# Two cross attentions of a Perceiver kernel: three score banks that small users borrow, row sums moved between engines, and a last head that ends by columns

## The reference, cut to what matters

```python
s = (q_h @ k_h.T) * scale            # 512 queries x 8192 keys; layer 0 also masks keys
p = exp(s - rowmax(s))
att_h = (p @ v_h) / rowsum(p)        # rowsum is called the denominator below
x = x + concat(att_h) @ Wo.T + bo
```

## Time and profile before

| | us |
|---|---|
| median of 3 runs | 4286.01 |
| lowest and highest | 4283.99, 4290.52 |
| the profiled execution's own time | 4285.99 |
| its span, first to last instruction | 4284.3 |
| PE busy | 3842.7 (90% of the span) |
| DVE busy | 2908.2 (68%) |
| ACT busy | 2380.9 (56%) |
| POOL busy | 1754.6 (41%) |

### The profile page before, as it was taken

The page is one execution under the profiler, slowest core; times in us unless marked ns, Lnnn a source line. Parts: engine busy times, 40 slices in busy tenths (PEclk is TensorE's granted clock), DMA queues, the critical chain, the costliest instruction groups (busy, mean ns, idle before and its releaser), DMA issues. The chain is left out here.

```text
span 4284.3 us, 51332 instructions
## 1 busy us (share of the span) xinstructions
PE 3842.7 (90%) x17864; PEld 2216.7 (52%) x17864; DVE 2908.2 (68%) x3503; ACT 2380.9 (56%) x3635; POOL 1754.6 (41%) x1064
## 2 busy tenths in 40 slices
PE   7998999999999677788999589999999988769996
PEld 6886444444444242366888344444444335447885
DVE  4333878778787269756888477877778644468886
ACT  2223777777777544225777146666666630337775
POOL 0000587787788639600000236666666630000001
PEclk9998999999999889889999689999999988779998
DMA  8996566666666520025889456666666541308886
GB/s 313 327 338 218 128 156 155 148 156 149 153 153 149 130 89 0 10 84 210 325 324 337 145 132 155 148 151 153 142 153 150 115 102 40 70 32 329 325 321 242
DMA packets 294234, 745.22 MB, mean 174 GB/s; under 512 B 55486, under 2 KB 89022, under 8 KB 259418
## 3 DMA queue, kind: packets, MB, share of 16 engines
q1 hardware_dynamic: 246522, 570.48, 39.7%
q0 software_dynamic: 47456, 171.46, 19.8%
HBM read 476.62 MB, written 99.48 MB: 134 GB/s over the span
## 5 line engine op out<-in xcount | busy, mean ns | idle before, releaser
L794 ACT ACTIVATE prob<-psum 128x512 f32<-128x512 f32 x1552 | 891.4, 595 | 430.5 <-PE psum L693 393.0
L963 POOL TENSOR_TENSOR den_pool<-den_pool,prob 128x1024 f32<-128x1024 f32 x372 | 938.6, 2523 | 221.7 <-DVE den_pool L881 189.7
L693 PE MATMUL psum<-q_stack,k_ring 98*128 98x512 f32 x2048 | 1006.0, 509 | 19.8 <-ACT prob L794 14.3
L852 DVE CUSTOM_DVE_ANT_0 psum<-psum,mask_q 128x1024 f32<-128x1024 f32 x512 | 626.4, 1234 | 222.7 <-PE psum L655 208.8
L848 DVE TENSOR_REDUCE row_max<-psum 128x1 f32<-128x1024 f32 x512 | 615.2, 1219 | 235.5 <-PE psum L655 232.3
L655 PE MATMUL psum<-k_ring,q_stack 96*128 96x512 f32 x2048 | 677.5, 414 | 62.6 <-DVE row_max L848 26.9
L693 PEld LDWEIGHTS psum<-q_stack,k_ring 98*128 98x128 f32 x2048 | 394.6, 193 | 617.3 <-ACT prob L794 274.5
L1984 DVE TENSOR_TENSOR weight_lo<-weight_raw,weight_hi 128x2048 fp32r<-128x2048 f32 x240 | 548.3, 2289 | 133.3 <-ACT weight_hi L1927 132.5
L711 PE MATMUL psum<-prob,x 128*32 128x512 f32 x3104 | 514.6, 609 | 0.9 <-ACT prob L794 0.9
L1927 ACT ACTIVATE weight_hi<-weight_raw 128x2048 fp32r<-128x2048 f32 x240 | 457.0, 1917 | 71.7 <-DMA weight_raw<-in_L_ffn_w 36.8
L655 PEld LDWEIGHTS psum<-k_ring,q_stack 96*128 96x128 f32 x2048 | 386.8, 196 | 152.9 <-issue 61.4
(11 more groups left out here) (428 smaller groups left out, 6420.6 us busy)
## 6 DMA issues: line engine op xcount, KB each, us to landing
weight_raw<-in_L_ffn_w SPq DMA_DIRECT2D x120, 1024.0 KB, 6.8
den_dma<-prob POOLq DMA_DIRECT2D x204, 512.0 KB, 4.9
k_ring<-k_hi SPq DMA_DIRECT2D x1024, 64.0 KB, 2.1
weight_raw<-in_L_ffn_Wu SPq DMA_DIRECT2D x60, 1024.0 KB, 7.4
weight_raw<-in_L_ffn_Wd SPq DMA_DIRECT2D x60, 1024.0 KB, 6.6
den_dma<-xnT POOLq DMA_DIRECT2D x68, 512.0 KB, 4.9
k_ring<-k_lo SPq DMA_DIRECT2D x512, 64.0 KB, 2.2
ctxT<-in_ctxT SPq DMA_DIRECT2D x16, 1024.0 KB, 9.5
```

The source lines that it names most:

```text
L693: e.matmul(k.bank(b % 2), k_ring[:, n % kring, kt * P:(kt + 1) * P], q_stack[h % n_q][:], start=not masked, stop=True, skip_group_check=ma ...
L794: e.activation(prob[b // 2 % n_p][:, b % 2, :], k.bank(b % 2), ACT.Exp, scale=scale).then_inc(s_exp, 1)
L852: e.tensor_tensor_reduce(out=max_banks(q), in0=max_banks(q), in1=masks[0][:, i, 2 * c2 * KC:2 * (c2 + 1) * KC], scale=1.0, scalar=-3.0e38, ...
L963: e.tensor_tensor(den[:], den[:], tile, ALU.add).then_inc(s_dpool, 1)
```

## The change

In its own words: "Cross attention: three score banks, shared with PE's sums of six tiles a head in layer 1, where VectorE adds none; last head's sums by PE; its end by columns". A class `Banks` hands out banks 0, 1 and 7 in order of use. Blocks rotate over three; while `out` (`head_out`), `sums` (the new `sum_wave`) or `rows` (`max_rows`) holds one, blocks have two: blocks 22 to 25, in layer 1 also 30 to 41, and 60 to 63 of each head. Waves are all of four value products again, 16 a head. In layer 1 each of waves 6, 7 and 8 is followed by a group of four products with ones; ScalarE takes their bank into `den_pe` (`take_sums`); VectorE adds no tiles there; transfers carry 9 tiles in place of 8, POOL 17 in place of 13, and the ring of `prob` tiles has 16 in place of 10. In the last head of either layer PE also sums the last four waves. The final projection is split around `head_out` and its last quarter follows four reciprocals of 128 columns each. The diff, cut:

```diff
+WAVES = KT // 4
+OUT_STEP, OUT_BACK = 10, 26
+ROWS_STEP, ROWS_BACK = PAIRS - 3, KT
...
+class Banks:
+    def __init__(self, banks, first, sums):
+        self.bank, self.user_before = {}, {}
+        self.free_at, self.used = dict.fromkeys(banks, 0), {n: -3 + j for j, n in enumerate(banks)}
+        self.user = dict.fromkeys(banks)
+        self._take(("rows", 0), 0, 0, first)
+        for b in range(H * KT):
+            h, t = divmod(b, KT)
+            waves = sums.pe_waves(h)
+            if t == 2 * OUT_STEP + 2 and h > 0:
+                self._take(("out", h - 1), b, KT * h + OUT_BACK)
+            if waves and t == 2 * wave_step(waves[0]) + 2:
+                self._take(("sums", h), b, KT * h + 2 * wave_step(waves[-1]) + 6 if h + 1 < H else KT * H + 1)
+            if t == 2 * ROWS_STEP + 2 and h + 1 < H:
+                self._take(("rows", h + 1), b, KT * h + ROWS_BACK)
+            self._take(("block", b), b, 0)
+        self._take(("out", H - 1), H * KT, 0)
+    def _take(self, user, b, back, n=None):
+        if n is None:
+            n = min((n for n in self.user if self.free_at[n] <= b), key=lambda n: self.used[n])
+        self.bank[user], self.user_before[user] = n, self.user[n]
+        self.user[n], self.free_at[n], self.used[n] = user, back, b
...
+    def pe_waves(self, h):
+        return self.waves if h + 1 < H else self.last_waves
+    def by_dma(self, h):
+        return self.dma_tiles if h + 1 < H else self.last_dma_tiles
+    def by_pool(self, h):
+        return [p for p in range(PAIRS) if p not in self.by_dve and p not in self.by_dma(h) and p // 2 not in self.pe_waves(h)]
...
-    n_q, n_p = 3, 7 if masked else 10
+    n_q, n_p = 3, 7 if masked else 16
...
-        sums = Sums([0, 1, 2, 3, 4], [], list(range(5, PAIRS - 2, 3)))
+        sums = Sums([0, 1, 2, 3, 4], [], list(range(5, PAIRS - 2, 3)), [12, 13, 14, 15], [5, 8, 11, 14, 17, 20, 23])
     else:
-        sums = Sums([0, 1, 2, 3, 4], [12, 15, 18, 21, 24, 27], [7, 10, 13, 16, 19, 22, 25, 29])
-    waves = Waves(sums.by_pe)
+        sums = Sums([], [6, 7, 8], [1, 4, 7, 10, 19, 22, 25, 28, 30], [6, 7, 8, 12, 13, 14, 15], [1, 4, 7, 10, 19, 22])
+    banks = Banks((0, 1, 7), 7, sums)
...
+    def wait_for_bank(e, kind, n):
+        if banks.user_before[kind, n] is None:
+            return
+        kind, n = banks.user_before[kind, n]
+        if kind == "block":
+            e.wait_ge(s_exp, n + 1)
+        elif kind == "out":
+            e.wait_ge(s_dsum, n + 1)
+        elif kind == "sums":
+            e.wait_ge(s_pesum, pe_sums(n))
+        else:
+            e.wait_ge(s_mlo, n + 1)
...
-                elif b >= 2:
-                    e.wait_ge(s_exp, b - 1)
+                else:
+                    wait_for_bank(e, "block", b)
...
+                if w in sums.pe_waves(h):
+                    sum_wave(h, w)
+            def sum_wave(h, w):
+                first, last = sums.pe_waves(h)[0], sums.pe_waves(h)[-1]
+                if w == first:
+                    wait_for_bank(e, "sums", h)
+                for n in range(4):
+                    t = 4 * w + n
+                    ins = e.matmul(bank_of("sums", h)[n * DH:(n + 1) * DH, :], k.ones[:, 0:DH],
+                                   prob[(PAIRS * h + t // 2) % n_p][:, t % 2, :], start=w == first, stop=w == last,
+                                   skip_group_check=True)
+                ins.then_inc(s_sumw, 1)
...
+                if sums.pe_waves(h):
+                    e.wait_ge(s_pesum, pe_sums(h))
+                    e.matmul(out[3 * DH:4 * DH, :], k.ones[:, 0:DH], den_pe, start=True, stop=True)
...
+            def project(i):
+                matmuls(e, k.bank(2 + i), [(attT[:, c, i * P:(i + 1) * P], wo[:, c, :]) for c in range(DT - 1)],
+                        stop=False)
+            project(0)
+            project(1)
+            head_out(H - 1)
+            project(2)
+            project(3)
             for i in range(TT):
-                matmuls(e, k.bank(i), [(attT[:, c, i * P:(i + 1) * P], wo[:, c, :]) for c in range(DT - 1)],
-                        stop=False)
-            head_out(H - 1)
-            e.wait_ge(s_rec, 8 * (H // 4 - 1) + 2)
-            for i in range(TT):
-                e.matmul(k.bank(i), attT[:, DT - 1, i * P:(i + 1) * P], wo[:, DT - 1, :], start=False, stop=True
+                e.wait_ge(s_rec, 8 * (H // 4 - 1) + 2 * i + 2)
+                e.matmul(k.bank(2 + i), attT[:, DT - 1, i * P:(i + 1) * P], wo[:, DT - 1, :], start=False, stop=True
...
+            def take_sums(h):
+                if h > 0:
+                    e.wait_ge(s_head, h)
+                e.wait_ge(s_sumw, sums.pe_done(h, sums.pe_waves(h)[-1]))
+                e.activation(den_pe, bank_of("sums", h), ACT.Copy, scale=1.0 / DH).then_inc(s_pesum, 1)
...
+                if h + 1 < H and sums.waves and p == wave_step(sums.waves[-1]):
+                    take_sums(h)
...
-                e.tensor_tensor(den4[g, :], den4[g, :], misc[2 * DH:3 * DH, :], ALU.add).then_inc(s_dsum, 1)
+                out = bank_of("out", h)
+                if sums.pe_waves(h):
+                    e.tensor_tensor(den4[g, :], den4[g, :], out[3 * DH:4 * DH, :], ALU.add).then_inc(s_dhalf, 1)
+                    e.wait_ge(s_dhalf, pe_sums(h))
+                e.tensor_tensor(den4[g, :], den4[g, :], out[2 * DH:3 * DH, :], ALU.add).then_inc(s_dsum, 1)
...
-            reciprocal(H // 4 - 1, 0, slice(0, T))
-            divide(H // 4 - 1, 8 * (H // 4 - 1) + 1, slice(0, T))
+            for i in range(TT):
+                reciprocal(H // 4 - 1, 0, slice(i * P, (i + 1) * P))
+                divide(H // 4 - 1, 8 * (H // 4 - 1) + 2 * i + 1, slice(i * P, (i + 1) * P))
...
-                if m == 1 and not sums.by_dve:
+                den, tiles = den_pool[h % 2], sums.by_pool(h)
+                e.wait_ge(s_exp, 2 * (PAIRS * h + p) + 2)
+                if p == tiles[1] and not sums.by_dve:
                     if h >= 2:
                         e.wait_ge(s_head, h - 1)
-                    e.tensor_tensor(den[:], prob[(PAIRS * h + sums.by_pool[0]) % n_p], tile, ALU.add
-                                    ).then_inc(s_dpool, 1)
+                    e.tensor_tensor(den[:], prob[(PAIRS * h + tiles[0]) % n_p], tile, ALU.add).then_inc(s_dpool, 1)
                     return
-                if m == 0:
+                if p == tiles[0]:
```

More of the change, by code:

```diff
@@ L457, with __init__ @@
 class Sums:
-    def __init__(self, by_dve, by_pe, by_dma):
-        self.by_dve, self.by_pe, self.by_dma = by_dve, by_pe, by_dma
-        self.by_pool = [p for p in range(PAIRS) if p not in by_dve and p not in by_pe and p not in by_dma]
+    def __init__(self, by_dve, waves, by_dma, last_waves, last_by_dma):
+        self.by_dve, self.waves, self.last_waves = by_dve, waves, last_waves
+        self.dma_tiles, self.last_dma_tiles = by_dma, last_by_dma
         self.dve_adds = max(0, len(by_dve) - 1)
@@ L559, in cross_attention @@
     den_dma = k.sbuf(ctx, "den_dma", [P, 2, T], F32)
+    den_pe = prob[(PAIRS * (H - 1) + 24) % n_p][:, 0, :] if not sums.waves else k.sbuf(ctx, "den_pe", [P, T], F32)[:]
     den4 = k.sbuf(ctx, "den_of_4_heads", [P, T], F32)
@@ L584, in chunk_cols, with bank_of, pe_sums @@
         return slice(c * KC, (c + 1) * KC)
+    def bank_of(kind, n):
+        return k.bank(banks.bank[kind, n])
+    def pe_sums(h):
+        return h + 1 if sums.waves else int(h + 1 == H)
+    def wait_for_bank(e, kind, n):
[10 more added lines that the diff above has]
+            e.wait_ge(s_mlo, n + 1)
     def max_banks(q):
@@ L694, in scores @@
+                e.matmul(out, k_ring[:, n % kring, kt * P:(kt + 1) * P], q_stack[h % n_q][:],
                          start=not masked, stop=True, skip_group_check=masked and b % 4 == 2).then_inc(s_score, 1)
             def wave(h, w):
-                blocks, summed = waves.values[w], waves.sums[w]
-                for t in blocks:
-                    if t % 16 == 0:
-                        e.wait_ge(s_v[t // 16], 16 * (h + 1))
+                if w % 4 == 0:
+                    e.wait_ge(s_v[w // 4], 16 * (h + 1))
@@ L701, in wave @@
                 if w == 0 and h > 0:
                     e.wait_ge(s_osb, h)
-                e.wait_ge(s_exp, KT * h + blocks[-1] + 1)
-                if summed is not None:
-                    if summed == waves.to_sum[0] and h > 0:
-                        e.wait_ge(s_dsum, h)
-                    e.matmul(misc[2 * DH:3 * DH, :], k.ones[:, 0:DH],
-                             prob[(PAIRS * h + summed // 2) % n_p][:, summed % 2, :],
-                             start=summed == waves.to_sum[0], stop=False, skip_group_check=True)
@@ L728, in waves_after @@
+                e.matmul(out[2 * DH:3 * DH, :], k.ones[:, 0:DH], den_pool[h % 2][:, 1, :], start=True, stop=True
+                         ).then_inc(s_head, 1)
             def waves_after(h, p):
-                for w in range(waves.count):
```

(9 more changed lines are left out.)

98 lines of the change are left out of this document (53 added, 45 removed).

## The result

The changed kernel takes 4249.26 us (median of 4 runs, 4246.73 to 4252.84) against 4285.14 (4 runs, 4283.99 to 4290.52): a ratio of 0.9914, 95% interval 0.9897 to 0.9932. It is 36 us faster, where 74 were forecast, and outside the range. Nearly half of the gain is there; most of the other half was spent inside layer 1.

A forecast was written before the change was run, and what follows sets the result against it. PE's own list plus the two-bank ring's wait was taken to bound layer 1. Layer 1's heads 54, layer 0's end 14.6 and layer 1's end 5.8 sum to 74.4, so 4286.0 becomes 4211; 8-in-10 range 4190 to 4240.

The forecast's parts named there:

- The third bank: Layer 1's scores: no more two-bank wait of 0.24 per four blocks over 11 periods, 2.7 us a head gained.
- VectorE's adds and the sum groups: Layer 1: a wait of 1.0 a head for VectorE goes; placing PE's sums behind waves gains 0.3.
- the port's and `take_sums`' losses: Layer 1, per head: 0.3 lost to copies waiting for the shared port, 0.1 to `take_sums` on ScalarE.
- An ordinary head: Layer 1, heads 0 to 14: 3.6 us less a head, 60.1 becomes 56.5, 54 in all.
- The ends from projection to last add: Both layers' ends become 16.0 us long, from 27.6 in layer 0 and 23.6 in layer 1.
- `max_rows` waiting for the copy: Layer 1: VectorE's tiny copy of the tops waits for POOL's add, stalling 0 to 1.1, mean about 0.3 a head.
- Division cost stays about as it is (three heads of fourteen): Layer 1's heads where VectorE divides: no change in cost, though one product had taken 3.27 while POOL added.
- the shared port lies on the path: Rival: each copy of the tops waits 2.4 and PE with it, 31 us lost, 4243; chance 0.07.
- does not set the pace: Layer 1: POOL's list of 55.6 a head stays below PE's 56.5, so POOL does not bound the head.
- The slack before `head_out`: Layer 1: merge issued some 7 us into the next head, landing at 12, `head_out` at about 19; 6 to 7 spare.
- The rival with POOL as the bound: Rival: POOL's list sets layer 1's pace at 58.5 us a head, 4225; chance 0.17.
- the last heads: Last heads before their projections: layer 0 gains 3 (bounds 0 and 6), layer 1 loses 1.8 by four more sum groups.

The follow-up runs named there:

- 4: Layer 1's scores back to two banks, its other users on the third alone, against the changed kernel: 4267.70 us, ratio 0.9941.
- 10: Layer 1's scores back to two banks, other users on the third alone, against kernel 8: 4249.97 us, ratio 0.9891.
- 7: Changed kernel with layer 1's DMA tiles moved: one transfer less, two adds between merge and first transfer: 4226.87 us, ratio 0.9837.
- 1: Changed kernel with the twelve middle products of layer 1's divisions left out, reciprocals kept: 4237.85 us, ratio 0.9866.
- kernel 8: 7 plus layer 1's division reciprocals at pairs 12 to 15, products at 16 to 19 of heads 4, 8, 12: 4207.04 us, ratio 0.9793.

## Why the prediction was wrong

**Right.** The third bank: 2.7 a head forecast, 2.8 measured twice (4 and 10). VectorE's adds and the sum groups: 0.9 a head forecast, with the port's and `take_sums`' losses taken off, 60.1 - 58.8 = 1.3 measured by 4. An ordinary head: 56.5 forecast, 55.9 measured. Layer 0's heads: 0 and 0.5. The ends from projection to last add: 16.0 forecast, 1475.12 - 1458.61 = 16.5 and 3450.44 - 3433.93 = 16.5 measured. `max_rows` waiting for the copy: 0.3 a head forecast, 2.2 in all over the fifteen measured, half of that.

**Wrong, the largest: "Division cost stays about as it is (three heads of fourteen)".** It went from 11 to 34, 23 lost. The row was there: a product of 3.27 while POOL adds, and POOL was given a continuous list. The step priced the tiny copy of the tops by this wait and put the four products at no change. They stand close together between maxima, one of 1.15 to 1.23 in each pair of 3.07 / 2 = 1.54, where a pair had 3.33 / 2 = 1.67 before. Their own time grew by only 6.2, or 0.5 in 7; the price came from VectorE's smaller room, from long products in a row, and from the clock: 9.7 of waits went with 15 of half clock (7). Head 8 of the kernel before, at 67.4 with three long ones in a row, had shown the price of one such head, 7.3. The rival "the shared port lies on the path" had the mechanism and the wrong instruction; at 4243 it was the nearest of the rivals, for the copy's price, with a chance of 0.07 though it was called the likeliest way to lose; that its number is near is luck.

The Trainium skill's page "SBUF — State Buffer", section "Who interferes with whom", has the pair of ports locked for a whole instruction. The trace agrees: 0.27 between two adds, 2.72 under an add that began 0.13 earlier.

**Wrong: POOL "does not set the pace".** Its list was put at 55.6; saturated it takes 56.8 in a head without disturbance, 58.5 in the mean (1). In the first, 1.6 more is in the three landings: 5.3, 5.5 and 6.1 where 3 x 5.1 was taken. The slack before `head_out`, "6 to 7", was near none, since the merge is issued some 13 into a head and not 7; head 4 began at 2713.2, and POOL's timeline has:

```profile
2726.13 0.88 POOL L1018 DMA_DIRECT2D den_pool<-den_dma  x1 [2.45 <-DMA den_dma<-xnT]
```

Cost in the changed kernel: 9 us in the ordinary heads, hidden below the divisions' heads, that gave the list time. The rival with POOL as the bound had the right number for the list, 58.5 a head, though the prediction derives it from nothing.

**Wrong: the last heads.** Layer 1's was to lose 1.8 and lost 10.2 (79.0 - 23.6 = 55.4 up to the projection before, 65.6 after): 6.3 waiting for the merge, late by the weights' load and by GpSimd, then half clock. Layer 0's was to gain 3 and lost 2.8: the ring still bound it, and four groups of sums came on top.

**The sum.** The shortfall is 37 to 38: 22 in layer 1's heads (23 by products, 9 by merge and copy, less some 9 by the better ordinary head, 15 x 0.6), 9 at layer 1's end, 6 at layer 0's. The check of the reasons is kernel 8, which mends the first two by other places and one transfer less: its fifteen heads take 840.3. That its time, 4207, is 4 below the forecast is partly luck, since these heads are 18 below the forecast's 858.4 (it had kept the divisions' 11, and its ordinary head was 0.5 longer), while the two ends are still 12 over it.

## What to carry to other kernels

When an edit fills an engine's list, look at every instruction of the engine that shares its port, and first at those that stand in bursts; place them in the filled engine's remaining gap, or where their own engine has room. The price of such a wait is not its length but what it does to the engine that waits next. Count a chain of transfers landing by landing, with what stands between two of them: two adds moved below a landing, with one transfer less, gave 21 us here. And price a gain twice, once for the step where nothing goes wrong and once for the steps where a second engine is at its limit, since what is gained in the first moves the second over it.

## What the runs showed of the hardware

A stop of PE of 2.3 us was followed by a granted clock of 0.59, 0.50, 0.50 and 0.70 in four windows of 4 us (head 4 of the changed kernel), one of 2.5 by 0.59, 0.50 and 0.63 in three (7). The same list in layer 1's last head ran at full clock in some kernels and at half in others. Two profiled executions of the changed kernel differed by 16.8 us, 14.7 of it in the heads with divisions, where products meet adds.
